# Spare bf16 products between the slot sums of two graph layers

## The reference, cut to what matters

```
alpha = softmax over edges into dst of leaky_relu(score[src] + score[dst])
out   = segment_sum(xW[src] * alpha, dst) + bias
```

## Time and profile before

| what | value |
|---|---|
| runs | 2488.91, 2496.96, 2488.14 us |
| median | 2488.91 us |
| span of the profiled execution | 2493.9 us |
| PE busy | 1779.5 us, 71% |
| DVE busy | 1586.0 us, 64% |
| POOL busy | 1504.0 us, 60% |
| ACT busy | 1366.9 us, 55% |
| mean granted clock of PE | 0.770 |

### The profile page before, as it was taken

How to read it: one execution, slowest core, us unless ns; L and a number is a source line. 1 busy time by engine, 2 the same in 40 slices (tenths; PEclk the granted TensorE clock), 3 DMA queues, 4 the chain that set the end, 5 groups by cost and what they waited for, 6 DMA issues and landing times. The chain is left out here.

```text
span 2493.9 us, 43223 instructions
## 1 busy us (share of the span) xinstructions
PE 1779.5 (71%) x9241; PEld 1123.8 (45%) x9241; DVE 1586.0 (64%) x4409; ACT 1366.9 (55%) x5004; POOL 1504.0 (60%) x1648
## 2 busy tenths in 40 slices
PE   6267767676766277776776767558888887878874
PEld 5144445444444144444444444335555555555542
DVE  4466666666668155555554556657777777877777
ACT  3255565556556144334344446536676667767666
POOL 3666666666657556656656663626666666766663
PEclk9576676767678566667777677768999989989886
DMA  6644444445531334434433531323433433433331
GB/s 175 160 124 121 115 122 123 118 117 156 144 84 58 97 105 109 111 106 110 112 106 110 164 101 37 113 59 100 114 108 109 117 112 107 114 107 108 107 89 52
DMA packets 130635, 274.39 MB, mean 110 GB/s; under 512 B 39700, under 2 KB 65273, under 8 KB 130366
## 3 DMA queue, kind: packets, MB, share of 16 engines
q0 software_dynamic: 64128, 181.33, 26.9%
q1 hardware_dynamic: 61564, 86.45, 11.6%
q10 hardware_dynamic: 4699, 3.86, 0.6%
HBM read 255.00 MB, written 17.20 MB: 109 GB/s over the span
## 5 line engine op out<-in xcount | busy, mean ns | idle before, releaser
L1271 POOL DMA_INDIRECT rows<-table,index_all x1320 | 1287.8, 976 | 833.2 <-PE bank L1775 383.8
L1775 PE MATMUL bank<-rows,onehot 128*128 128x264 f32 (+1 forms) x2640 | 1089.8, 529 | 290.1 <-ACT rows L1481 156.3
L839 DVE TENSOR_TENSOR sums<-sums,bank 128x264 f32 (+1 forms) x1320 | 555.7, 421 | 465.8 <-PE bank L1775 202.8
L1481 ACT ACTIVATE rows<-rows,wgt 128x33 f32<-128x33 f32 (+2 forms) x3120 | 809.6, 344 | 1.2 <-issue 1.1
L1775 PEld LDWEIGHTS bank<-rows,onehot 128*128 128x128 f32 x2640 | 557.9, 247 | 461.7 <-issue 204.7
L1433 ACT CAST onehot<-bank 128x768 f32<-128x768 bf16 x240 | 177.7, 742 | 301.5 <-remote 174.4
L1489 ACT ACTIVATE prod<-bank 128x512 f32<-128x512 f32 x240 | 133.6, 557 | 244.5 <-PE bank L1787 126.2
L1794 PE MATMUL bank<-late,onehotT 128*128 x1320 | 202.1, 291 | 1.1 <-DVE prod L848 1.1
L848 DVE TENSOR_TENSOR prod<-prod,bank 128x512 f32<-128x512 f32 x240 | 152.4, 635 | 50.3 <-remote 27.4
L857 DVE TENSOR_REDUCE dots<-prod 128x16 f32<-128x512 f32 x240 | 151.7, 632 | 0.5
L1696 PE MATMUL bank<-identb,onehotT 128*128 128x128 bf16 x1320 | 138.3, 251 | 16.6 <-issue 10.0
(11 more groups left out here) (208 smaller groups left out, 2018.0 us busy)
## 6 DMA issues: line engine op xcount, KB each, us to landing
locb<-loc_d SPq DMA_DIRECT2D x120, 352.0 KB
rows<-table,index_all POOLq DMA_INDIRECT x1320
flags<-flags_d SPq DMA_DIRECT2D x508, 27.5 KB
table<-rows SPq DMA_DIRECT2D x25, 136.0 KB, 1.8
table<-rows SPq DMA_DIRECT2D x25, 134.0 KB
late<-table SPq DMA_DIRECT2D x1, 3300.0 KB
table<-rows SPq DMA_DIRECT2D x25, 129.5 KB, 2.3
late<-table SPq DMA_DIRECT2D x1, 3212.5 KB
```

The lines of the kernel that those rows point to most:

```text
L839: done(v.tensor_tensor(a, a, sum_bank(l, t, s)[:, 0:VV], ALU.add), "add")
L1271: g.indirect_dma_start(out=rows[:, t.u, s, 0:ROW[l]], out_offset=None, in_=table[l], in_offset=bass.IndirectOffsetOnAxis(ap=index_all[:, t ...
L1481: i = a.activation(r, r, ACT.Copy, scale=wgt[:, t.u, h * B + s:h * B + s + 1])
L1775: done(m.matmul(sum_bank(l, t, s)[:, 0:VV], onehot[:, t.u, s, :], rows[:, t.u, s, 0:VV], start=True, stop=True), "agg")
```

## The change

`sum_slot` gets two edits, both in layers 0 and 1 (the table for layer 2 is empty).

Ahead of certain slot sums PE issues a group of bf16 products: the bf16 identity as the stationary operand, 248 bf16 columns of the f32 identity as the moving one. Their results go into columns 264 to 511 of the bank that this slot's sum will use, which nobody reads. Layer 0 has 12 of them ahead of slot 4 and 8 ahead of slot 8; layer 1 has 10 ahead of slot 3, 8 ahead of slot 7 and 6 ahead of slot 9.

The wait for the bank (`need(pe, "add", ...)`) moves ahead of the wait for the weighted rows (`weighted`), and the group stands between the two.

```diff
+SPARE = ({4: 12, 8: 8}, {3: 10, 7: 8, 9: 6}, {})
...
+                def keep_busy(b, n):
+
+                    for _ in range(n):
+                        m.matmul(b[:, VMAX:512], identb[:, :], ident[:, :].bitcast(BF16)[:, 0:512 - VMAX],
+                                 start=True, stop=True)
+
                 def sum_slot(t, s, l=l, VV=VV):
                     i = (l * K + t.k) * B + s
                     if s == 0:
                         need(pe, "hotT", 2 * (l * K + t.k) + 2)
+                    need(pe, "add", i + 1 - len(ps_sum[l]))
+                    keep_busy(sum_bank(l, t, s), SPARE[l].get(s, 0))
                     weighted(pe, l, t.k, s)
-                    need(pe, "add", i + 1 - len(ps_sum[l]))
                     done(m.matmul(sum_bank(l, t, s)[:, 0:VV], onehot[:, t.u, s, :], rows[:, t.u, s, 0:VV],
                                   start=True, stop=True), "agg")
```

## The result

The changed kernel takes 2543.4 us (median of four runs, 2538.7 to 2544.4), the kernel before 2488.5 us in the runs beside it. The ratio on record is 1.020, with a 95% interval of 1.017 to 1.022 (the quotient of the two medians is 1.022; for the experiments too the ratios on record are given). The time was 23 us above the forecast of 2520 us, and inside the range. The profiled execution has a span of 2542.6 us, 48.7 us more than before, and PE's mean granted clock rose from 0.770 to 0.838.

A forecast was written before the change was run, and what follows sets the result against it. No engine was full, so a loop of waits was taken to bound layers 0 and 1. The sum 2493.9 + 30 + 3 = 2527 us of span became 2520 us; the range for 8 in 10 runs was 2462 to 2545.

The forecast's parts named there:

- Which side, and where: Whole kernel: slower, chance 0.60, through layer 1's eight products ahead of slot 7, on the path to POOL's second gathers.
- Remaining wait of 2.9 us behind slot 3: Layer 1: ten products leave 2.9 us of PE's 3.91 us wait idle, so the clock still falls in most batches.
- Price of a product: PE, each spare product of 248 columns: 0.10 us at the full clock, 0.21 us at the low one.
- Size of layer 1's term: Layer 1, first to second group of gathers: mean 7.56 us against 6.74, in 37 batches +30 us.
- the three kinds and their shares: Layer 1, first to second gather group: 8.56, 7.3 or 6.07 us by when the clock falls; shares 0.4, 0.4, 0.2.
- The rival with the low clock at slot 7 always: Layer 1: each of 37 batches pays 1.65 us more, +61 us, 2550 us; chance 0.07.
- From the span to the time: Whole kernel: profiled span of 2527 us times 0.998 gives a median of 2522 us, stated as 2520.
- Layer 0 at 0: Layer 0, groups ahead of slots 4 and 8: waits cover them, cost 0; +11 us if slot 8's cover fails.
- Ends of the layers +3: Last batches of layers 0 and 1, where PE is dense: groups lengthen the path by +3 us, at most 20.
- The moved wait at 0: Layers 0 and 1, wait for the bank ahead of the group: costs 0, since PE waited for both events before.
- The floor taken as it stands: Layers 0 and 1: first to second gather group takes at least about 6.05 us, whatever PE's clock; cause not fully told.
- Covered by POOL's wait ahead of the first group: Products behind slot 7 cost 0, hidden by POOL's wait of 2.12 us in layer 0, 1.88 us in layer 1.

## Why the prediction held, and what was off in it

**Which side, and where:** right. The loss sits in layer 1, in the stretch from the first to the second group, and comes from slot 7's group; leaving that group out lowered the ratio from 1.020 to 1.003, by the ratios 40 of the 49 us by which the kernel got slower, and the group alone gave 1.018.

**Remaining wait of 2.9 us behind slot 3:** right. It is 2.96 us in the batch shown, and 2.6 to 3.0 us in nearly all. The clock falls within it in one batch of three and behind slot 4's sum in the others, "only more often late" as forecast. Twenty products in that wait, ahead of slot 4, kept the clock at 1.00. What the Trainium skill says in TensorE: Matmul & The Clock Gate, section "What's actually happening", that activity releases the throttle, agrees with that run and with the rise of the mean clock from 0.770 to 0.838; but the 24 products of a batch kept the clock up through slot 7 in no batch of layer 1 after the first. That section says nothing on what the time becomes.

**Price of a product:** close at both clocks. Ten took 1.22 us at the full clock (predicted 1.05) and twenty 2.28 us (2.1 in the expectation of that run), eight 1.86 us at the low one (1.65).

**Size of layer 1's term:** too small, +30 us forecast and +41 us measured in the batches. The step that failed is the three kinds and their shares. I gave one batch in five the floor of 6.07 us, at a clock that holds through slot 7; only the first batch had it. The shares were a choice, and two errors in them partly offset each other by luck: the longest kind was 8.28 us and not 8.56, with a third of the batches and not 0.4, while the fastest fifth was missing. With 7.07, 8.01 and 8.28 in equal parts the mean is 7.79 us. That gives 7.79 - 6.74 = 1.05 us in each of 37 batches, 39 us.

**The rival with the low clock at slot 7 always:** I gave it 0.07, and its condition is what the trace shows: in each of the 36 batches of layer 1 after the first the eight products begin at the low clock. Its 2550 us is also nearer to the 2543 measured than my 2520. It is too high because a batch paid 1.0 us more on average and not 1.65: in two of three kinds slot 4's sum was fast, and in two of three the clock came back by slot 7's sum (0.60 and 0.80 us instead of 1.23).

**From the span to the time:** the forecast span of 2527 us was 16 us below the measured 2542.6. Of these, 13 lie in layers 0 and 1 (45.9 us more instead of 33) and 3.3 in the lead-in, which no edit touches and which moves between 116.9 and 121.6 us among the profiles. I then took off 7 us, since the kernel before had a median 5 us below its profiled span and by rounding; here the median and the span agree within 1 us.

**Layer 0 at 0:** nearly. The stretch stayed at 6.10 us (before it lay between 5.94 and 6.11 us over the batches, a little wider than I had read), the layer took 3.5 us more here and 7.4 us in the run with its groups alone. A faster clock gave it nothing, as the floor said.

**Ends of the layers +3:** from the start of the last batch but one to the next layer's first batch it took 124.1 us behind layer 0 and 148.7 us behind layer 1, against 123.9 and 147.0, +1.9 us.

**The moved wait at 0:** right. Layer 1 takes 794.5 us in the run with layer 0's groups alone and layer 0 takes 752.9 and 752.8 us in the two runs with products in layer 1 alone; these layers have the moved wait and no products, and before they took 795.3 and 753.6 us.

**The floor taken as it stands:** it held in layer 0 with either clock, and it is no property of the sums. With five gathers in the first group it moved from 6.05 to 7.5 us in half of the batches of layer 0. On the second kind of chip the wait isn't there at all. Runs of the first kind show where such a floor can come from: some of PE's results reach ACT and DVE 2 to 4 us and POOL 1 to 2 us after the profile has their product ended. In layer 1 this ends for most of them together, about 1.5 us after the last gather of a run was issued; in layer 0 of the changed kernel also within a run of gathers. The trace can't tell a late signal from an instruction that ran late, since it models the ends of matmuls; and why the cast comes at once in one kernel and 3.7 us late in the next stays open.

**Covered by POOL's wait ahead of the first group:** I argued that products behind slot 7 cost nothing as long as that wait of 1.88 to 2.12 us holds. For six ahead of slot 9 and ten ahead of slot 3 it did (1.003 as a whole). With eight more ahead of slot 8 it didn't: +33 us in layer 1 in the profiles. A cover read from a wait counts only if every reader behind it stays on time. My theory after the first runs, that the place ahead of slot 7 alone decides, falls with that run.

## What to carry to other kernels

Filling PE's idle time raises its clock, and it pays only where the filler stands inside a wait and the work that another engine waits for comes behind it at the full clock: twenty products in the wait ahead of slot 4 gave -0.5%, eight of them right ahead of the sum that releases POOL's gathers +1.8%. Read the filler's price at the low clock too, for that is what it costs when the clock has fallen, as it had at slot 7 in every batch of layer 1 but the first. And try such an edit on more than one chip: one that is worth half a per cent on one cost 2% on another.

## What the runs showed of the hardware

The same kernel took 2487 to 2490 us on some chips and 2099 us on others. The engines' instructions last the same on both (a gather's issue 0.98 and 0.97 us, DVE's add 0.42 us); what differs is how long after PE's products the other engines go on, 0.03 us on the one and 3.5 us on the other for the same scan, and so how much POOL waits for the sums in layers 0 and 1. On the slower kind most of it ends about 1.5 us after the last of a run of POOL's indirect gathers. No run here tells what in the chip makes the difference.

A wait of PE of 2.96 us had the clock low at the next sum in one batch (1.20 us for the pair); after waits of 2.95 and 2.57 us in the two batches before, the next sum still ran at the full clock (0.67 us for the pair), and the clock fell behind it. So the length of the wait alone didn't decide. Twenty bf16 products of 2.28 us in the wait kept the clock at 1.00 in 33 of 37 batches.
